# Two expert stages of a hybrid layer: the load of the second weight table is issued ahead of the rows and the output bias

## What is computed

```python
x = x + mamba(layernorm(x), ...)
x = x + ffn(layernorm(x), Wr, W1, b1, W2, b2)
x = x + causal_attention(layernorm(x), w_q, w_k, w_v)
x = x + ffn(layernorm(x), Wr, W1, b1, W2, b2)

def ffn(x, Wr, W1, b1, W2, b2):        # E = 8 experts, K = 2, C = 256, H = 1024
    probs = softmax(x @ Wr)
    topk_probs, topk_experts = top_k(probs, 2)
    # every token goes to its two experts, at most 80 of a batch row to one expert
    buf[e, b, pos] = x                                   # routed rows
    h = relu(einsum('ebnc,ech->ebnh', buf, W1) + b1)
    y = einsum('ebnh,ehc->ebnc', h, W2) + b2
    return sum over the two experts of y[e, b, pos] * topk_prob
```

## Time and profile before

| | us |
|---|---|
| median of 3 runs | 3229.64 (3225.42 to 3231.66) |
| the profiled execution | 3236.31 |
| its span, first to last instruction | 3234.5 |
| expert stage ffn1, about | 1708 to 2206 |
| expert stage ffn2, about | 2697 to 3234 |

### The profile page before, as it was taken

How to read it: one execution, slowest core, us unless ns; L and a number is a source line. 1 busy time by engine, 2 the same in 40 slices (tenths; PEclk the granted TensorE clock), 3 DMA queues, 4 the chain that set the end, 5 groups by cost and what they waited for, 6 DMA issues and landing times. The chain is left out here.

```text
span 3234.5 us, 54379 instructions
## 1 busy us (share of the span) xinstructions
PE 2880.0 (89%) x16992; PEld 2285.2 (71%) x16992; DVE 2343.9 (72%) x4219; ACT 1760.0 (54%) x3332; POOL 2186.3 (68%) x1405
## 2 busy tenths in 40 slices
PE   5899989999899898999857999996999985999998
PEld 2566666666666665666547999996777775999998
DVE  2998889888898888988965666564566654666564
ACT  3766767667676566766534444452333333444443
POOL 2888988889888898899955555552233435565554
PEclk8999999999999999999978999997999997999999
DMA  4231222112221122211244445442222223444443
GB/s 106 104 112 67 81 74 71 45 55 81 75 73 42 55 81 76 72 44 53 74 159 137 115 105 129 94 116 53 76 85 85 89 80 111 116 111 110 105 116 48
DMA packets 192660, 281.60 MB, mean 87 GB/s; under 512 B 35943, under 2 KB 164622, under 8 KB 184264
## 3 DMA queue, kind: packets, MB, share of 16 engines
q1 hardware_dynamic: 157128, 236.31, 22.1%
q0 software_dynamic: 35328, 42.76, 7.4%
HBM read 197.28 MB, written 94.72 MB: 90 GB/s over the span
## 5 line engine op out<-in xcount | busy, mean ns | idle before, releaser
L605 POOL TENSOR_TENSOR dbu<-du,bb 128x1024 f32<-128x1024 f32 x512 | 1198.1, 2362 | 66.2 <-DVE hs L755 63.0
L755 DVE TENSOR_TENSOR_SCAN hs<-da,dbu 128x1024 f32<-128x1024 f32 x512 | 1145.4, 2275 | 49.4 <-POOL dbu L605 20.9
L690 ACT ACTIVATE da<-delta 128x512 f32<-128x512 f32 x1024 | 571.3, 595 | 270.2 <-DVE hs L755 249.4
L855 PEld LDWEIGHTS yT<-ident,hs 128*128 128x128 f32 x4096 | 501.7, 150 | 162.3 <-issue 115.1
L855 PE MATMUL yT<-ident,hs 128*128 128x128 f32 x4096 | 552.2, 288 | 27.4 <-DVE hs L755 27.2
L1322 POOL TENSOR_TENSOR ffn_w_lo<-ffn_w,ffn_w_hi 128x512 fp32r<-128x512 f32 x256 | 344.1, 1370 | 177.8 <-ACT ffn_w_hi L1317 173.6
L1368 PE MATMUL ffn_hbank<-ffn_rowsT_hi,ffn_w_hi 128*128 128x320 f32 x1024 | 341.4, 333 | 43.7 <-DVE ffn_hT_lo L1390 41.5
L1402 PE MATMUL ffn_ybank<-ffn_w_hi,ffn_hT_hi 128*128 128x256 f32 x1280 | 365.1, 285 | 0.7 <-DVE ffn_hT_lo L1390 0.7
L1404 PE MATMUL ffn_ybank<-ffn_w_hi,ffn_hT_lo 128*128 128x256 f32 x1280 | 359.5, 281 | 0.0
L1403 PE MATMUL ffn_ybank<-ffn_w_lo,ffn_hT_hi 128*128 128x256 f32 x1280 | 359.3, 281 | 0.0
L1370 PE MATMUL ffn_hbank<-ffn_rowsT_hi,ffn_w_lo 128*128 128x320 f32 x1024 | 322.2, 315 | 0.0
(11 more groups left out here) (237 smaller groups left out, 5271.1 us busy)
## 6 DMA issues: line engine op xcount, KB each, us to landing
bb<-b_rows SPq DMA_DIRECT2D x64, 1024.0 KB, 4.5
ffn_w<-L_ffn_W SPq DMA_DIRECT2D x64, 1024.0 KB, 10.1
slots<-empty SPq DMA_DIRECT2D x40, 530.0 KB, 6.5
ffn_rows<-slots SPq DMA_DIRECT2D x32, 662.5 KB, 5.0
a_x<-x_after_mamba SPq DMA_DIRECT2D x32, 512.0 KB
xt<-L_attn_a_x SPq DMA_DIRECT2D x16, 512.0 KB
x<-L_attn_a_x SPq DMA_DIRECT2D x16, 512.0 KB, 4.1
x_after_mamba<-x SPq DMA_DIRECT2D x16, 512.0 KB, 2.9
```

The costliest lines, as they stand in the source:

```text
L605: pool.tensor_tensor(dbu[:, s % DEEP], du[:, dt, :].unsqueeze(1).to_broadcast([P, SN, T]), bb[:, q * SN:(q + 1) * SN, :], ALU.mult).then_i ...
L690: ins = act.activation(da[:, s % 2, i, :], delta[:, par, dt, :], ACT.Exp, scale=-float(q * SN + i + 1))
L755: dve.tensor_tensor_scan(flat[0], flat[1], flat[2], 0.0, ALU.mult, ALU.add).then_inc(scanned.sem, 1)
L855: mm = pe.matmul(yT[:, j * P:(j + 1) * P], hs[:, s % DEEP, i, j * P:(j + 1) * P], k.ident[:], start=False, stop=(q == QS - 1 and i == SN - ...
```

## The change

In `load` the step for `w2`, with its wait, is taken out from behind the rows and `b2` and put ahead of them. The first two turns of a stage are taken out of the loop: turn 0 keeps the old order, turn 1 has the new one. The loop over the other turns of the first half starts at 1. All other engines' programs are the same.

```diff
+        def load(sp, turn, par, e):
+            load_w1(sp, turn, par, e)
+            load_w2(sp, turn, e)
+            load_rows(sp, turn, par, e)
...
-                with sp.Fori(0, E // 2) as pair:
+                load_w1(sp, 0, 0, 0)
+                load_rows(sp, 0, 0, 0)
+                load_w2(sp, 0, 0)
+                load(sp, 1, 1, 1)
+                with sp.Fori(1, E // 2) as pair:
                     for par in range(2):
                         load(sp, pair * 2 + par, par, pair * 2 + par)
```

More of the change, by code:

```diff
@@ L1290, in experts, with load_w1, load_rows @@
         y_mm, y_part, y_ev = (Count(sem(n), NR, ahead=2) for n in ("y_mm", "y_part", "y_ev"))
-        def load(sp, turn, par, e):
+        def load_w1(sp, turn, par, e):
             sp.wait_ge(w_lo.sem, w_lo.at(turn - 2, WP))
             sp.dma_start(w1[:, par], w["W1"][e].rearrange("(k p) h -> p k h", p=P)).then_inc(w1_loaded[par].sem, 16)
+        def load_rows(sp, turn, par, e):
             sp.wait_ge(y_ev.sem, y_ev.at(turn - 2, NR))
@@ L1298, in load, with load_w2 @@
                 sp.dma_start(dst, src).then_inc(loaded[par].sem, 16)
+        def load_w2(sp, turn, e):
             sp.wait_ge(w_lo.sem, w_lo.at(turn - 1, 2 * WP))
             sp.dma_start(w2[:], w["W2"][e].rearrange("(m p) c -> p m c", p=P)).then_inc(w2_loaded.sem, 16)
+        def load(sp, turn, par, e):
+            load_w1(sp, turn, par, e)
+            load_w2(sp, turn, e)
+            load_rows(sp, turn, par, e)
         def weight_piece(piece, par):
```

## The result

| | us |
|---|---|
| median before (4 runs) | 3229.08 (3225.42 to 3231.66) |
| median after (4 runs) | 3171.32 (3170.18 to 3172.08) |
| ratio on record, after to before | 0.9824, 95% interval 0.9812 to 0.9836 |
| profiled execution before, its span | 3236.31, 3234.5 |
| profiled execution after, its span | 3170.18, 3168.4 |

The change saves 57.8 us at the medians. Between the two profiled executions it is 66.1 us, mostly because the profiled execution before lies 7.2 us above its median.

The account below looks back on a forecast made before the run. The late second table was taken to bound the expert stages through ScalarE, VectorE and TensorE. Gains of 45.4 and 14.4 less 0.5 give 59.3 us, from median 3229.6 to 3170.3, stated as 3171; range 3163 to 3190, about 0.8.

Parts of the forecast that it names:

- What bounds the kernel: Expert stages: ScalarE waits for the second table's DMA 14 times a stage, which holds up VectorE, then TensorE.
- Why the table was late: SyncE's queue: second table issued behind the rows, about 2904.7, though its own wait was over at 2889.6, 15 us earlier.
- First term: Turns 1 to 14 of both stages: VectorE's waits behind the late table vanish, gain 45.4 us.
- Second term: TensorE's clock in the expert stages: nine half-clock stretches after its pauses vanish, 1.6 us each, gain 14.4 us.
- Third term: Turn 0 of each stage: turn 1's rows and bias now queue behind the second table, loss 0.5 us, bounds 0 to 5.
- What costs nothing: SyncE's eight more instructions and the table's transfer beside GpSimd's scatters, with DMA engines 16% busy, were claimed free.
- The stretches stay: Rival on TensorE's clock: half-clock stretches have another cause and remain, gain only 44.9 us, 3184.7 us; chance 0.24.
- Slower, because TensorE works without rest: Rival: without pauses TensorE's clock falls more often, two stretches a turn, 3260 us; chance 0.04.
- The turn that should take 29.8 us: Sign of success: the turn from 2872.59 to 2903.61, 31.0 us before, would take 29.8 us.

Follow-up runs that it names:

- the table last of four: Against the kernel before, each turn loads rows, bias, first table of the turn after, then second table: 3334.05 us, ratio 1.0329.
- six banks: Changed kernel with the first product running through six PSUM banks, TensorE up to six jobs ahead of VectorE instead of four: 3165.16 us, run again 3165.47 us.
- The order alone: Changed kernel, but the second table, still ahead of the rows, waits for the end of turn t - 2 as they do: 3172.47 us, ratio 0.9826.
- six copies: Changed kernel plus six idle ScalarE copies at step 4 of turns 0 to 14, ahead of the weight piece: 3265.53 us, ratio 1.0117.
- four and five copies: Changed kernel plus four or five idle ScalarE copies at step 4 of turns 0 to 14: 3203.30 us with four, 3216.20 us with five.

## Why the prediction was right

The forecast was 3171 us, the measured median is 3171.32. That they agree to 0.3 us is luck: run again, the same kernel had a median of 3174.24 us. Its steps:

- **What bounds the kernel.** Right. The chain was table, ScalarE, VectorE, TensorE: with the table on time TensorE has next to no idle time left in the turns, and with it made later the time grows (the table last of four). It was not all that there was to gain, though. TensorE reads as busy for 451.64 of 452.00 us, and six banks still save 8.8 us: its first matmul of jobs 13 to 15 reads as 0.41 us instead of 0.31 and stands at VectorE's pace, a limit that the busy time hides.
- **Why the table was late.** Only half right. The forecast says that the load that could go at 2889.6 goes at 2904.7, and rests the cure on those 15 us. The order alone, with the table leaving at the end of the turn, gives the same time. What cost the time was the transfers ahead of it in the queue. The forecast had the rows for this, since it named the four loads that go out together.
- **First term, 45.4 us.** Right in size: the turns' waits are gone, and what is gained, 46.0 us by the table of turns, is VectorE's wait and not ScalarE's 73.5 us. Together with the second term it is 59.7 us in the profiled executions, where the forecast has 59.8.
- **Second term, 14.4 us.** The mechanism holds: pauses made without a late load bring stretches, and without pauses there are none. A stretch cost 1.50 and 1.54 us where 1.6 was taken. But the number of stretches came from one execution, and its nine are more than another trace with the same order has (five), so the term can be 6 us smaller in another execution. The sum was taken off the median all the same. It is 59.3 us against the medians' 57.8, a difference that is within the scatter of the runs; what made it is not shown.
- **Third term, 0.5 us.** It was zero. In turn 0 the bias went out at 2681.93 and landed 7.9 us later, at 2689.8:

```profile
DMA to landing us min/median/max: 7.9/7.9/7.9
...
2692.26 1.03 PE L1340 MATMUL ffn_tbank<-ident,ffn_rows 128*128 128x128 f32 x8
```

 TensorE came for the rows at 2692.26, 2.4 us after, and did not wait.
- **What costs nothing.** Right: the table's transfer beside the scatters is not to be seen in any wait of TensorE.
- **The rivals.** "The stretches stay" rested on the page TensorE: Matmul & The Clock Gate of the Trainium skill, by whose section on HAM oscillation pauses as short as these leave the clock alone. The runs don't agree: 30 pauses of 1.89 us on average, the longest 2.24, brought 21 stretches. "Slower, because TensorE works without rest" is out as well: in 451.64 busy us of 452.00 the clock was 1.00. The turn that should take 29.8 us takes 29.9 to 30.2, two lengths by turns, which the forecast, worked out from one turn, did not see.

## What to carry to other kernels

Where one queue issues several loads at the same moment, read for each when it is wanted after its issue and when it lands: the one with the least slack goes first, and here no earlier issue was needed. Count a removed wait by the engine that is the slowest behind it (here VectorE, 45 us), not by the one that the view of waits names (ScalarE, 73 us). Look at the granted clock just behind a pause of TensorE: with pauses of 1.8 to 1.9 us a stretch of half clock cost 1.5 us more. And do not take an engine that reads as busy all the time for one that can go no faster: compare the spacing of its jobs with the pace of the engine that it hands them to.

## What the runs showed of the hardware

- A pause of TensorE of about 1.9 us in work that is otherwise dense is in two cases of three (21 of 30, six copies) followed, within 2 us, by 3.4 us at 1.2 GHz, and such a stretch cost 1.5 us. 60 pauses of 0.84 and 1.36 us on average (four and five copies) brought none, and 28 of 3.7 us (the table last of four) brought 28 stretches, half of them of 6.8 us.
- Of four loads issued together the landing depends on the place. The bias of 128 KB lands 6.8 us after its issue as the second (before), and 9.4 us after as the third, behind a table of 1 MB and the rows (the order alone). The table of 1 MB landed 9.1 us after its issue as the third and 6.9 us after as the first, in one turn of each of these kernels.
